# A post-norm transformer stack on one core: the order of work inside an attention step

## The reference, cut to what matters

```
x = layernorm(x + attention(x))        # 8 sequences of 256 tokens, width 256, 16 heads of 128, causal
x = layernorm(x + experts(x))          # 32 experts, 6 per token, and a shared one
x = layernorm(x + state_space(x))
x = layernorm(x + grouped_experts(x))  # 16 experts, 4 per token, and a shared one

attention: q, k, v = x W_Q, x W_K, x W_V
           pattern = softmax(mask(q k^T / sqrt(128)))
           out     = sum over heads of (pattern v) W_O
```

## Time and profile before

| | us |
|---|---|
| median of 3 runs | 1674.98 |
| the profiled execution | 1677.12 |
| its span | 1675.2 |
| PE busy in the span | 1617.7 (97%) |
| a steady group of the attention (95.28 to 168.16) | 72.88 |
| PE, DVE, ACT, POOL busy in it | 70.25, 58.95, 46.82, 19.80 |

### The profile page before, as it was taken

The page is one execution under the profiler, slowest core; times in us unless marked ns, Lnnn a source line. Parts: engine busy times, 40 slices in busy tenths (PEclk is TensorE's granted clock), DMA queues, the critical chain, the costliest instruction groups (busy, mean ns, idle before and its releaser), DMA issues.

```text
span 1675.2 us, 29756 instructions
## 1 busy us (share of the span) xinstructions
PE 1617.7 (97%) x9992; PEld 1414.1 (84%) x9992; DVE 1140.4 (68%) x2889; ACT 767.0 (46%) x1897; POOL 627.3 (37%) x379
## 2 busy tenths in 40 slices
PE   7999999999999889999999999999999999999997
PEld 6988888898888878888888888888888888888886
DVE  5878878787887765556567578748784857753633
ACT  5666666665665543435333444335333533323221
POOL 2322223232222004323467225841675147533232
PEclk9999999999999999999999999999999999999999
DMA  6434434344342026657665556655655466555663
GB/s 214 156 139 142 153 116 175 138 141 153 126 166 110 1 90 200 191 186 214 200 214 181 172 186 206 196 186 158 205 185 175 146 194 196 177 179 175 191 207 107
DMA packets 101498, 278.28 MB, mean 166 GB/s; under 512 B 13488, under 2 KB 17584, under 8 KB 100368
## 3 DMA queue, kind: packets, MB, share of 16 engines
q1 hardware_dynamic: 101392, 276.91, 51.2%
HBM read 230.23 MB, written 46.63 MB: 165 GB/s over the span
## 4 chain that ended last, share of the span: by engine, by line
PE 59%; DVE 15%; issue 15%; POOL 6%; ACT 4%; DMA 1%; SPq 0%; POOLq 0%; DVEq 0%; ACTq 0%
PE psum L334 53%; POOL act_sb L551 4%; PE psum L1293 2%; DVE s_sb L991 1%; PE psum L1304 1%; DVE conv L1098 1%; POOL mix L573 1%; DVE act_lo L1057 1%; ACT p_sb L674 1%; PE psum L1480 1%; PE psum L1283 1%; ACT kT_hi L633 1%; DVE s_sb L989 1%; DVE kT_lo L885 1%; DVE stats L892 1%
## 5 line engine op out<-in xcount | busy, mean ns | idle before, releaser
L334 PE MATMUL psum<-xT_hi,gu_w 128*128 128x512 f32 x1632 | 554.5, 400 | 1.3 <-DVE act_sb L1052 1.1
L551 POOL TENSOR_TENSOR act_sb<-act_sb,comb 128x512 f32<-128x512 f32 x184 | 310.2, 1686 | 627.6 <-DVE act_sb L1052 627.4
L714 ACT ACTIVATE gated<-psum 128x512 f32<-128x512 f32 x204 | 122.0, 598 | 618.9 <-PE psum L334 618.7
L1052 DVE TENSOR_TENSOR act_sb<-psum,gated 128x512 f32<-128x512 f32 x204 | 140.7, 690 | 380.9 <-PE psum L334 379.4
L334 PEld LDWEIGHTS psum<-xT_hi,gu_w 128*128 128x128 f32 x1632 | 307.7, 189 | 73.7 <-DVE act_sb L1052 3.0
L334 PE MATMUL psum<-xT_lo,gu_w 128*128 128x512 f32 x816 | 322.9, 396 | 0.0
L334 PEld LDWEIGHTS psum<-d_w,act_hi 128*128 128x128 f32 x1632 | 221.8, 188 | 18.6 <-issue 0.6
L517 POOL TENSOR_TENSOR split_stage<-raw_stage,split_stage 128x768 fp32r<-128x768 f32 x56 | 103.0, 1839 | 354.2 <-ACT split_stage L623 354.2
L334 PE MATMUL psum<-d_w,act_hi 128*128 128x256 f32 x1632 | 227.3, 282 | 0.4 <-ACT act_hi L722 0.4
L334 PEld LDWEIGHTS psum<-xT_lo,gu_w 128*128 128x128 f32 x816 | 153.9, 189 | 29.7
L1057 DVE TENSOR_TENSOR act_lo<-act_sb,act_hi 128x512 fp32r<-128x512 f32 x204 | 150.4, 737 | 1.8 <-ACT act_hi L722 1.8
(11 more groups left out here) (203 smaller groups left out, 3502.8 us busy)
## 6 DMA issues: line engine op xcount, KB each, us to landing
gu_w<-w_split SPq DMA_DIRECT2D x204, 512.0 KB, 3.6
d_w<-w_split SPq DMA_DIRECT2D x204, 256.0 KB, 3.8
w_split<-split_stage SPq DMA_DIRECT2D x56, 768.0 KB, 3.9
raw_stage<-w_all SPq DMA_DIRECT2D x56, 384.0 KB, 4.3
decay_all<-decay_dram SPq DMA_DIRECT2D x32, 384.0 KB, 5.2
in_w<-w_split SPq DMA_DIRECT2D x44, 256.0 KB, 4.1
aw_raw<-attn_w SPq DMA_DIRECT2D x8, 1024.0 KB, 6.3
comb<-l_comb_dram SPq DMA_DIRECT2D x128, 64.0 KB, 3.1
```

What stands on the lines that cost most here:

```text
L334: last = nc.tensor.matmul(out_ap, w, m, start=start and n == 0, stop=stop and n == len(pairs) - 1, **kw)
L551: pool.tensor_tensor(act_sb[:, s % 2, :], act_sb[:, s % 2, :], comb[:, comb_block(s) % 2, :], ALU.mult).then_inc(comb_done, 1)
L714: act.activation(gated[:, s % 2, :], psum[:, G_BANK, :], ACT.Silu).then_inc(gated_ready, 1)
L1052: dve.tensor_tensor(act_sb[:, s % 2, :], psum[:, U_BANK, :], gated[:, s % 2, :], ALU.mult).then_inc(t_ready, 1)
```

## The change

In the loops of three engines two blocks change places within a step. No instruction is added or taken out.

- ACT: `pT_last` and `pT_hi` of unit i-2 come ahead of the high part of the first job.
- DVE: `pT_lo` of unit i-2 comes ahead of the low part of the first job.
- PE: the turns of unit i-2 come directly after the scores of unit i, ahead of the first job.

```diff
@@ ACT @@
-                    for bp, j in jobs:
-                        qkv_high(g, bp, j)
                     if u_t is not None:
                         u = u_t
                         act.wait_ge(pT_ready, g * UNITS + u + 1)
                         act.activation(pT_last[:, u % 2, :], psum[:, PT_BANK, 2 * P:3 * P], ACT.Copy)
                         act.activation(pT_hi[:, u % 2, :], psum[:, PT_BANK, 0:2 * P], ACT.Copy).then_inc(pT_hi_ready, 1)
+                    for bp, j in jobs:
+                        qkv_high(g, bp, j)
@@ DVE @@
-                    for bp, j in jobs:
-                        qkv_low(g, bp, j)
                     if u_t is not None:
                         u = u_t
                         dve.wait_ge(pT_hi_ready, g * UNITS + u + 1)
                         dve.tensor_tensor(pT_lo[:, u % 2, :], psum[:, PT_BANK, 0:2 * P], pT_hi[:, u % 2, :].bitcast(F32),
                                           ALU.subtract).then_inc(pT_lo_ready, 1)
+                    for bp, j in jobs:
+                        qkv_low(g, bp, j)
@@ PE @@
                     if u_s is not None:
                         scores(g, u_s)
+                    if u_t is not None:
+                        transposes(g, u_t)
                     for bp, j in jobs:
                         qkv_job(g, bp, j)
-                    if u_t is not None:
-                        transposes(g, u_t)
```

## The result

The changed kernel takes 1689.08 us, the median of four runs between 1688.56 and 1690.04, against 1675.55 for the kernel before in the same comparison. The ratio is 1.008, with a 95% interval of 1.0068 to 1.0092: slower by 13.5 us, where +12.4 and 1687.4 us were forecast. The profiled execution took 1688.56 us with a span of 1686.6.

A forecast was written before the change was run, and what follows sets the result against it. PE, busy 97% of the span, was taken as the bound, waiting in attention only for DVE. Seven groups at +1.60 us (11.2) plus 1.2 for the last gave +12.4, 1687.4 us; forecast's own range 1683 to 1692, 8-in-10 range 1676 to 1696.

The forecast's parts named there:

- Step 2: Attention group, turns of unit 0: PE waits 1.55 us for DVE's scaling L999; the next scores come 0.97 us later.
- Steps 3 and 4: Attention group: later `kT_lo` leaves values +0.19 us; then turns wait 0.43 us for `pT_lo`, shift +0.62 us.
- Steps 5 to 11: Attention steps with jobs, values and outputs: no new wait, no gain; shift stays +0.62 us, tightest margin 0.3 us.
- Step 12: Attention step without a job: turns wait 0.23 us for `pT_lo`, values 0.76 us for `zT_lo`; shift stays +0.62 us.
- Step 13: Attention group: turns wait 1.10 us for `pT_lo` with the q job still to do; values +1.72 us.
- Step 16: Attention group, turns of unit 14: wait 0.67 us, shift +0.20; k job now behind them, shift +1.60 us.
- The sum: Whole kernel: +1.60 us a group, 11.2 for seven groups, 1.2 for the last; +12.4 us.
- The last group: Final attention group, without POOL operations or jobs in steps 13 to 18: 1.2 us taken between bounds 0 and 2.5.
- the waits just go: Rival: PE's waits of 1.4 and 0.8 us vanish in all 8 groups, 17.6 us faster, 1657.4 us; chance 0.10.
- only the early steps pay: Rival: PE regains the 1.40 us of step 16, leaving +0.62 x 8 = 5 us, 1680.0 us; chance 0.15.
- DVE becomes the bound: Rival: DVE steps wait for ACT's two extra copies and lags add up, 23 us slower, 1698 us; chance 0.08.

The follow-up runs named there:

- the run with the small operation: Full change, with POOL's low part of weight blocks cut to 8 elements from the second group on; 1684.67 us, ratio 1.0051 to the kernel before.
- PE alone: Kernel before with only PE's loop reordered, turns directly after scores, ACT and DVE as before; 1710.23 us, ratio 1.0208.
- the copies alone: Kernel before with only ACT's and DVE's loops reordered, PE's order as before; 1682.82 us, ratio 1.0044.

## Why the prediction was right

- **Step 2.** Forecast: turns released by the scaling, PE standing 1.55, scores of step 3 at +0.97. Measured: turns 0.05 behind the end of L999, the trace's wait 1.39 (it counts from the modelled end of the matmul before; by starts it is 1.53), scores at +0.98. That about a microsecond of it hangs on POOL is shown by the run with the small operation, where the turns come 1.01 earlier.
- **Steps 3 and 4.** Forecast +0.19, then +0.62. Measured +0.12 at the values of step 3, +0.04 at the scores of step 4, and +0.63 at those of step 5. The v job and the values of step 3, no longer beside the turns, took PE less time than I carried over from before, so the +0.19 was too high; the turns of step 4 then waited longer for the same `pT_lo`. The sum is set by DVE, and was right.
- **Steps 5 to 11.** No new wait: the shift is 0.63 to 0.67 throughout, and the run that changes only the steps from 5 on shows none in them.
- **Step 12.** The wait for `pT_lo` turned into one for `zT_lo`, 0.48 by the trace and 0.75 by starts, where 0.76 was forecast. Values and scores are no earlier, as said.
- **Step 13.** Forecast a wait of 1.10 and +1.72 at the values; measured 1.11 by starts, +1.86 at the values and +1.77 at the scores of step 14.
- **Step 16.** Forecast turns +0.20, group +1.60; measured +0.33 and +1.64. DVE's mask of step 15 was 0.1 later than I made it.
- **The sum.** 11.2 for seven groups, measured 11.81. The last group got 1.2; from its start to the first expert matmul the after trace has 79.5 us, the two traces of before 78.7 and 78.1, so 0.8 to 1.4. The 1.2 was picked between wide bounds, not worked out, so its fit is in part luck. The rest of the 13.5, under a microsecond, is below what the runs tell.
- **The rivals.** That the waits just go fell at steps 2 and 13. That only the early steps pay is refuted by the run that changes the later ones alone. That DVE becomes the bound would have had to show a growing shift in steps 5 to 11, and there is none in the full change; with PE's part alone it does appear there, 0.9 us a group.

What the prediction didn't have: that the two halves depend on each other. PE alone costs 4.76 a group, the copies alone 0.70, together 1.69. Walking the steps for the whole change doesn't give that, and my expectations for the halves were off: PE alone by 1.3 a group above the upper end, the copies alone by 0.8 (-0.1 expected as the sum of its two terms).

## What to carry to other kernels

When an operation that waits is moved ahead of independent work, first ask what that work covered: the wait is paid in every step in which the releaser isn't there yet, even where before it showed no wait at all. A wait that the profile puts on one operation at the end of another engine's step can be a wait for that whole step, as in steps 12 and 16 here; then moving the one operation up hands the wait to the next one needed, so move all that the waiting engine needs next, and fill the releasing engine's own idle time with the rest. Put the order right on the engine that is late, in the steps where it is late, and leave the cover of the engine that bounds.

## What the runs showed of the hardware

A DVE scaling of 128x128 fp32 took 0.29 us by itself and 1.32 beside a POOL operation of 1.82 that had started 0.57 earlier, ending with it to 0.07. Cutting that POOL operation to 8 elements took the scaling to 0.29 at the same place. Yet of the 6.1 us by which DVE's busy time in a group fell (59.48 to 53.40) only 0.8 reached the length of the group: in this kernel the hold-up cost time only where DVE's chain was the last thing that PE waited for.
